# The adjacency mask goes through TensorE, and the leaky slope is split between ScalarE and VectorE

## What is computed

```python
e = src[:, :, None] + dst[:, None, :]          # h = layernorm(x), Wh = h W^T, src = Wh a1, dst = Wh a2
e = jnp.where(e > 0, e, 0.2 * e)
e = jnp.where(adj > 0, e, -9e15)
attention = jax.nn.softmax(e, axis=-1)
x = x + jnp.einsum('bij,bjf->bif', attention, Wh)
```

## Time and profile before

| | |
|---|---|
| median of 3 runs | 456.99 us (456.24 to 458.05) |
| the profiled execution, its own time | 457.38 us |
| span of its profile | 455.6 us |
| PE busy | 372.8 us, 82% |
| DVE busy | 259.4 us, 57% |
| ACT busy | 224.3 us, 49% |
| POOL busy | 259.4 us, 57% |

### The profile page before, as it was taken

The page is one execution under the profiler, slowest core; times in us unless marked ns, Lnnn a source line. Parts: engine busy times, 40 slices in busy tenths (PEclk is TensorE's granted clock), DMA queues, the critical chain, the costliest instruction groups (busy, mean ns, idle before and its releaser), DMA issues.

```text
span 455.6 us, 11418 instructions
## 1 busy us (share of the span) xinstructions
PE 372.8 (82%) x2965; PEld 347.3 (76%) x2966; DVE 259.4 (57%) x997; ACT 224.3 (49%) x564; POOL 259.4 (57%) x283
## 2 busy tenths in 40 slices
PE   2779879877866868952999999994399999999991
PEld 1558758656755757852999999994299999999991
DVE  2599999998787766730444444442044444444451
ACT  1358856575652644430545555552055555555540
POOL 5123124856872147777777666666037665776663
PEclk9999999999877876995999999998589999999996
DMA  3254325544654514946998877846667676676610
GB/s 99 81 162 133 113 81 147 180 141 151 194 189 165 152 37 151 274 172 206 312 297 280 261 257 257 274 169 202 173 192 223 213 237 216 209 232 219 227 35 0
DMA packets 75546, 83.34 MB, mean 183 GB/s; under 512 B 10564, under 2 KB 60111, under 8 KB 75504
## 3 DMA queue, kind: packets, MB, share of 16 engines
q1 hardware_dynamic: 66032, 61.58, 44.3%
q0 software_dynamic: 9472, 21.26, 13.3%
HBM read 36.06 MB, written 28.94 MB: 143 GB/s over the span
## 4 chain that ended last, share of the span: by engine, by line
PE 47%; DVE 18%; issue 13%; POOL 8%; DMA 5%; SPq 4%; ACT 3%; POOLq 0%; DVEq 0%; ACTq 0%
PE bank L487 23%; PE bank L497 11%; POOL out_dram L1027 6%; PE bank L364 5%; DVE h L678 3%; DVE stats L668 2%; DMA shared<-in_adj_dram 2%; ACT R L546 2%; DVE R L731 2%; PE bank L410 2%; PE bank L412 2%; POOL sorted_rows L1005 2%; SPq L296 1%; DVE shared L708 1%; PE bank L418 1%
## 5 line engine op out<-in xcount | busy, mean ns | idle before, releaser
L487 PE MATMUL bank<-xT,w_t 128*128 128x128 f32 x1280 | 173.8, 280 | 2.5 <-issue 1.0
L487 PEld LDWEIGHTS bank<-xT,w_t 128*128 128x128 f32 x1280 | 160.0, 197 | 3.7 <-issue 3.6
L927 DVE TENSOR_TENSOR prob<-em,bank 128x256 f32<-128x256 f32 x160 | 67.4, 421 | 134.1 <-ACT em L612 99.5
L612 ACT ACTIVATE em<-bank 128x256 f32<-128x256 f32 x160 | 61.3, 384 | 110.8 <-PE bank L487 106.3
L1027 POOL DMA_INDIRECT out_dram<-R x80 | 78.6, 982 | 54.5 <-issue 30.6
L497 PE MATMUL bank<-W,prob 128*128 x640 | 98.1, 277 | 2.4 <-DVE prob L927 1.3
L1027 POOL DMA_INDIRECT sorted_rows<-R x80 | 78.7, 984 | 31.6 <-issue 27.4
L497 PEld LDWEIGHTS bank<-W,prob 128*128 128x128 f32 x640 | 84.5, 193 | 3.0 <-issue 3.0
L996 POOL TENSOR_TENSOR rstd<-var_eps,half_neg 128x4 f32<-128x4 f32 x32 | 32.6, 1028 | 85.0 <-DVE var_eps L684 85.0
L1005 POOL DMA_INDIRECT sorted_rows<-R,ROW x64 | 64.7, 1012 | 18.4 <-issue 17.5
L364 PE MATMUL bank<-ident,R 128*128 128x128 f32 x224 | 37.9, 296 | 44.0 <-DMA R<-sorted_rows 25.5
(11 more groups left out here) (124 smaller groups left out, 371.5 us busy)
## 6 DMA issues: line engine op xcount, KB each, us to landing
R<-sorted_rows SPq DMA_DIRECT2D x160, 130.0 KB
w_t<-W SPq DMA_DIRECT2D x80, 256.0 KB, 2.4
W<-in_L_ffn_w_dram SPq DMA_DIRECT2D x48, 128.0 KB, 3.1
sorted_rows<-pad SPq DMA_DIRECT2D x34, 130.0 KB, 2.3
R<-in_x_dram SPq DMA_DIRECT2D x16, 256.0 KB, 3.0
shared<-in_adj_dram SPq DMA_DIRECT2D x16, 256.0 KB, 3.8
sorted_rows<-R POOLq DMA_INDIRECT x80
out_dram<-R POOLq DMA_INDIRECT x80
```

The source lines that it names most:

```text
L487: ins = nc.tensor.matmul(H[k][:, m * P:(m + 1) * P], w_t[:, par, k, m * P:(m + 1) * P], xT[:, par, k * P:(k + 1) * P], start=True, stop=True)
L612: nc.scalar.activation(sil[:, k % 2, :], H[k][:, 0:HC * P], ACT.Silu).then_inc(silu_ready, 1)
L927: V.tensor_tensor(hidT[:, k, :], sil[:, k % 2, :], H[k][:, HC * P:2 * HC * P], ALU.mult).then_inc(hid_ready, 1)
```

## The change

The mask tile becomes bf16, 1 where there is no edge and 0 where there is one. TensorE adds it into the scores by one more product, of `barred` (the identity times -4.5e16, made once by GpSimd) and `mask`, at the end of the accumulation in bank `E`. The operation that made `em` on VectorE is gone. ScalarE writes `em = 0.4 |E|` from PSUM instead, and VectorE's slope is `lr = 0.6 E + em`, which is the same as the leaky slope of 0.2. TensorE waits for `lr` rather than `em` before it overwrites the bank.

```diff
-        mask, lr, Wh = shared[:, 0:2, :], shared[:, 2:4, :], shared[:, 4:6, :]
+        mask = shared[:, 0:1, :].bitcast(BF16).rearrange("p a (b n) -> p (a b) n", b=2)
+        lr, Wh = shared[:, 2:4, :], shared[:, 4:6, :]
...
                     if later(i, 1):
-                        pe.wait_ge(em_ready, i)
-
+                        pe.wait_ge(lr_ready, i)
                     nc.tensor.matmul(E[:], dst_w[:], hT[:, par, :], start=True, stop=False)
                     for g in range(GG):
-                        ins = nc.tensor.matmul(E[:, g * N:(g + 1) * N], hT[:, par, g * N:(g + 1) * N], src_w[:],
-                                               start=False, stop=(g == GG - 1))
-                    ins.then_inc(e_done, 1)
+                        nc.tensor.matmul(E[:, g * N:(g + 1) * N], hT[:, par, g * N:(g + 1) * N], src_w[:],
+                                         start=False, stop=False)
+                    pe.wait_ge(mask_ready, i + 1)
+                    nc.tensor.matmul(E[:], barred[:], mask[:, par, :], start=False, stop=True).then_inc(e_done, 1)
...
                     if later(i, 2):
-                        act.wait_ge(em_ready, i - 1)
-
-                    nc.scalar.activation(mask[:, par, :], adj_t[:, par, :], ACT.Relu, scale=2 * MASKED).then_inc(mask_ready, 1)
+                        act.wait_ge(e_done, i - 1)
+
+                    nc.scalar.activation(mask[:, par, :], adj_t[:, par, :], ACT.Relu, scale=-1.0, bias=1.0).then_inc(mask_ready, 1)
...
+                    act.wait_ge(e_done, i + 1)
+                    if later(i, 1):
+                        act.wait_ge(lr_ready, i)
+                    nc.scalar.activation(em[:], E[:], ACT.Abs, scale=(1 - SLOPE) / 2).then_inc(em_ready, 1)
...
-                if has(1):
-                    dve.wait_ge(e_done, i)
-                    dve.wait_ge(mask_ready, i)
-                    if later(i, 2):
-                        dve.wait_ge(lr_ready, i - 1)
-
-                    V.scalar_tensor_tensor(em[:], mask[:, 1 - par, :], -MASKED, E[:], ALU.add, ALU.min).then_inc(em_ready, 1)
...
-                    V.scalar_tensor_tensor(lr[:, 1 - par, :], em[:], SLOPE, em[:], ALU.mult, ALU.max).then_inc(lr_ready, 1)
+                    V.scalar_tensor_tensor(lr[:, 1 - par, :], E[:], (1 + SLOPE) / 2, em[:], ALU.mult, ALU.add).then_inc(lr_ready, 1)
...
+            g.tensor_scalar(barred[:], ident[:], -MASKED, None, ALU.mult).then_inc(const_steps, 1)
```

More of the change, by code:

```diff
@@ L85, in gat_moe_kernel @@
         ones_bf = sb("ones_bf", [P, P], BF16)
+        barred = sb("barred", [P, P], BF16)
         e_before = sb("e_before", [P, NE, NE])
@@ L351, in _ @@
             pe.wait_ge(small_in, 80)
-            pe.wait_ge(const_steps, 11)
+            pe.wait_ge(const_steps, 12)
             pe.wait_ge(setup_v, 1)
@@ L657, in carry @@
             def carry():
-                dve.wait_ge(const_steps, 17)
+                dve.wait_ge(const_steps, 18)
             def row(i, g):
@@ L986, in _ @@
             g.memset(e_jump[:, NE - 1:NE], float(2 * ZBLK)).then_inc(const_steps, 1)
-            pool.wait_ge(const_steps, 15)
+            pool.wait_ge(const_steps, 16)
             g.tensor_scalar(e_up[:], t_n[:, 0, :], -0.498, None, ALU.add).then_inc(const_steps, 1)
```

## The result

Over six runs each, the changed kernel takes 452.08 us (449.46 to 454.12) and the kernel before 458.27 us (456.24 to 459.02). The ratio is 0.9869, with a 95% interval of 0.9828 to 0.9910. So the change takes 6.0 us off, with bounds of 4.1 and 7.9. The profiled execution took 451.82 us with a span of 450.1, against 457.38 and 455.6.

What follows compares the result with a forecast made beforehand. VectorE was taken to set the pace until about 166 us, with a fixed tail after. 0.24 + 0.60 + 0.04 + 3.60 - 1.33 = 3.15 us off 457.38 gives 454.2, or 453.9 on the median's scale; range 450.8 to 457.0.

Steps and rivals of the forecast that it cites:

- three signs by which the prediction was to be wrong: Slope waits for modulus beyond the last group; number of half-clock stretches on the path differs; tail behind the dispatches changes.
- The tail: From GpSimd's last 32 dispatches on: length unchanged, VectorE's gain until 166 us passed on one to one, first dispatch near 162.9.
- 0.60 each in the exposed iterations: Iterations 7, 8, 10 to 15: choose, place or table steps outlast the root, so removing L698 counts in full, 0.60 us.
- leads of my sum: Time gained over the kernel before, carried through the iterations: 0.24 to the end of iteration 6, 0.84 after 7, about 0.88 after 9.
- The wall in iterations 8 and 9: Attention products of group 6, with 0.63 us of slack, meet iteration 8's 0.60; net of both iterations +0.04 us.
- The cover in plain iterations: Iterations 2 to 6 and 9: h waits for GpSimd's root, so the removal yields 0.1 us instead of 0.6.
- The mask product: TensorE, 16 products: 0.22 us each at full clock, 0.40 at half; on the path in iterations 11, 13, 14, 15, together -1.33.
- The modulus: ScalarE, 16 times, nearest row 584 ns: fits in 0.68 before Wh's copy, costs nothing beyond the 0.22.
- The clock: TensorE's half-clock stretches at 121, 132 and 147 us lie on the path; the sum left them as they were.
- with the clock as it was: The prediction's own case: its sum with unchanged half-clock stretches, 452.8 to 455.2 us, 48%.
- the clock decides: Rival: number of half-clock stretches on TensorE's path changes, 1.7 us per stretch of 3.4; more favourable 17%, less favourable 15%.
- one less, 452.2: Within the clock rival: one half-clock stretch fewer on the path gives 452.2 us; more favourable clock 17%.

Runs made afterwards that it cites:

- e2: Changed kernel with an operation like the removed one put back ahead of h in iterations 7, 8 and 10 to 15; 0.9961 of the kernel before.
- e5: Kernel before with only VectorE's part: L698 gone, one operation left, no mask product, no modulus; 0.9834 of the kernel before.
- e1: Changed kernel with an operation like the removed one put back ahead of h in iterations 1 to 6, 9 and 16; 0.9892 of the kernel before.
- e3: Changed kernel without the 16 mask products, the wait for the mask tile kept; 0.9829 of the kernel before.
- e4: Changed kernel with each modulus on ScalarE done twice, the first into a tile nobody reads; 0.9904 of the kernel before.
- e7: Changed kernel with idle products on TensorE ahead of its waits for h and the second normalisation and of each count; 0.9821 of the kernel before.
- e8: Changed kernel with VectorE's shift put ahead of the slope operation; 0.9796 of the kernel before.
- e6: Kernel before with idle products on TensorE ahead of its waits for h and the second normalisation and of each count; 0.9905 of the kernel before.
- e9: Changed kernel as it stands, run again on a chip that is 85 us slower; 0.9934 of the kernel before there.

## Why the prediction was right, and where it was off

The range held, but the point of it did not: 3.1 us were forecast and 6.0 measured. Two of the three signs by which the prediction was to be wrong came true: the slope waited for the modulus in more than the last group, and the half-clock stretches on the path are one fewer than before. Term by term:

*The tail,* one to one from the first of 32 dispatches: right, 289.6 and 289.9 us. The first dispatch was said to come near 162.9 and came at 160.23.

*0.60 each in the exposed iterations:* right in size. e2 and e5 price the operation by itself, at 0.58 to 0.61. From group 7 to 13 the leads of my sum grow by 2.22 us (0.84 to 3.06); the traces show 2.00.

*The wall in iterations 8 and 9:* there, but not where I had it. My sum took 0.56 of the 0.60 back at the attention products. In the trace the lead grew by 0.84 up to h of group 9, and then the load of adj in iteration 9, which VectorE awaits for 1.45 us, took the whole lead of 1.41. By h of group 10 it had grown by 0.45 over h of group 7, where my sum had 0.64. That the two totals are close is luck.

*The cover in plain iterations:* right in kind. h waits for the root seven times, 4.7 us in all, and e1 puts eight operations back for about 1 us. The lead at h of group 7 was said to be 0.84 and was 0.57. It passed 1.0 at h of group 6 (50.38 against 51.41) and the late load took half of it back. In the traces whose VectorE list is the same that far (changed, e3, e4, e7), h of group 7 came at 60.55 to 61.86. So this term moves by over 1 us from one trace to the next, and it was given too finely. At h of group 2 these four differ by 1.4 us already; the loads are not all of it.

*The mask product:* 0.22 us at full clock, as said, and 0.21 us less in the step behind iteration 11 without it. For half clock 0.40 was said; in e8's trace Wh starts 0.43 us behind the product there.

*The modulus:* hidden, as said, but "the slope has it nearly an iteration early, except for group 15" was not whole. VectorE waited for it twice: 1.5 us for group 15, and 3.1 for group 0, where it cost nothing, since the slope still came at 18.84 against 19.47 before.

*The clock:* here the sum was mis-sized. My case was "with the clock as it was", and the term of mask products in iterations 13 to 16 was -1.11, two of them priced at half clock. Between h of group 13 and the dispatch the sum gained 0.09 us (two removals, 1.20, less products of 0.40, 0.40 and 0.31), and the traces show 3.23 gained. Of this, 2.00 came between h of groups 13 and 14 and 1.21 between 14 and 15, where 0.2 each were expected. In iteration 13 the score group took 1.92 us before and 1.05 after; in iteration 14 it took 1.92 and then 1.61. e6 parts the first of these two steps: with VectorE's work as before and iteration 13 at full clock, it is 1.62 us quicker there than the kernel before. That leaves 0.38 of the 2.00 for the change itself, which is one removal less one product at full clock.

That is the rival "the clock decides", with 17% against my own case's 48%, and the stretch that it lost is one of those it named. That its "one less, 452.2" is also the measured time is luck in part. It stood for 4.8 us below the 456.99 of the kernel before; over six runs that kernel came out at 458.27, and 6.0 were measured.

Whether the change brings this or luck does is only half settled. In the traces of the changed kernel and of e1 to e8 the scores of iteration 13 all run at full clock (1.05 us), e6 included, whose VectorE list is that of before. In three traces (e1 with 1.69 us, e5 with 1.81, and the repeat e9 with 1.92) iteration 12 is slow instead. There is one trace of the kernel before. But the granted clock of every execution is on record, as a mean over its span. In the 28 executions of the kernel before that count in the sets of e1 to e8, it is 0.919 on average. It is 0.924 in the six of the changed kernel, 0.925 to 0.931 in each of e1, e3, e4, e5 and e8, none of which has the mask step, and 0.922 in e2, which has most of that work back where it counts. So without that step TensorE runs a little less at half clock, and this isn't the luck of one trace alone. The mean doesn't tell how much of that time lies on the path.

Shown is: without the clock the change is worth about 3 us, by 2.95 us in the steps up to h of group 14 (0.57, 2.00 and 0.38), and half-clock stretches cost the kernel before some 4 us (e6). The nearest to both kernels at one clock are e6 and e7, on one chip: 0.9905 and 0.9821, 3.8 us apart, with an estimate of 2.8 either way from the scatter of their six runs each. Open is how much of the half-clock time on the path the change takes away on average.

## What to carry to other kernels

Before an operation is taken off the busiest engine, look at what the next one waits for once it is gone: here a 1.05 us root on another engine covered half of sixteen removals. Sixteen times the step of the removed operation would have given 9.6 us. A load that comes late can take a whole lead back, as the one in iteration 9 did with 1.41 us. And when the busy engine feeds a chain that it later waits for, the order of its instructions counts: a 0.15 us operation ahead of a 0.68 us one was worth about 3 us (3.3 in the changed kernel, and 2.8 in the kernel before, with bounds of 0.3 and 5.3), as much as the change itself without the clock.

## What the runs showed of the hardware

Products that nobody reads, put where TensorE waits, raised the granted clock and took 4.3 us off the kernel before: here the stretches at half clock were a cost of waiting, and it could be bought off.

One chip ran the same kernels in 542 us instead of 457. In e9 the first of the 32 dispatches starts at 166.2 us, 6.0 later than in the changed kernel's first profile, and from there to the end of the span it is 369.2 us instead of 289.9. So most of the 85 us lie in the later part. There ScalarE computes the silu of the mixture (L619, which shares the buffer `em` with the modulus). ScalarE's waits from 166 to 330 us (what waits for what: us in total, times, longest), of the changed kernel's first profile and then of e9:

```profile
ACT em L619 <- PE bank L490: 57.3, 79, 2.2
```

```profile
ACT em L619 <- PE bank L490: 55.3, 23, 4.3
ACT em L619 <- remote: 27.3, 4, 12.5
```

In the first profile it waits 79 times for the products L490, 0.7 us each; in e9 it waits 23 times, 2.4 us each, and four times more, 27.3 us in all, for something that the profile calls remote. One of the long ones:

```profile
249.93 1.06 PE L490 MATMUL bank<-xT,w_t 128*128 128x128 f32 x8
...
251.27 1.06 PE L490 MATMUL bank<-xT,w_t 128*128 128x128 f32 x8
...
253.09 0.38 ACT L619 ACTIVATE em<-bank 128x256 f32<-128x256 f32 x1 [3.85 <-PE bank L490]
```

Two product groups of 1.06 us run while ScalarE is idle for 3.85 us, and it starts 0.76 us after the second has ended, where the first profile has such starts within 0.12 us of a group's end. So the products are recorded as done and their reader is late. What is slow on that chip stays open.
